# A rank-one matmul for the output bias in place of a GpSimd addition, with the residual loaded into the output tile and the weight loads spread differently (8 cores, one Trainium2 chip)

## The chip, the cores and the metric

The kernel runs on the eight cores of one Trainium2 chip. Each core takes two of the 16 sequences and works alone; nothing is exchanged. The metric is the device time in microseconds (us) of the slowest core. Before the change the median of three runs is 1172.06 us (1171.53 to 1172.96).

TensorE (PE in the profile; PEld is its weight load) multiplies into banks of PSUM, DVE is VectorE, ACT is ScalarE, POOL is GpSimd, and SP is the sync engine that only starts DMAs. Each works through a list of its own in order; semaphores join the lists.

## The reference

One layer over x of shape 16 x 2048 x 1024, float32:

```
xn  = layernorm(x)                                  # no scale, no shift
# branch 1
n   = xn * rsqrt(max(sum(xn*xn), 1e-12))            # rows of length one
sim = n @ n.T                                       # 2048 x 2048 for each sequence
c   = softplus(sum(relu(sim), axis=-1) @ W1 + b1)   # 2048 x 1024
a   = concat([xn, c]) @ W2                          # W2 is 2048 x 1024
# branch 2
P   = xn @ U1                                       # rank 256
H   = gelu(P @ V1 + fb1)                            # 4096 wide
f   = H @ U2 @ V2 + b2
out = x + a + f
```

## The kernel before, in words

A core works on its two sequences ("batches" b = 0 and 1), each in four tiles of 512 tokens (t), each of four blocks of 128 tokens (s_; st = 4t + s_ numbers the 16 blocks). All matmuls are in bfloat16 and mostly 512 columns wide.

An operation is recorded by `A(stream, ...)` with what it reads and writes; `Sched` derives the semaphore waits and appends it to the list of its engine: T is TensorE, V is DVE, S is ACT, G is GpSimd, SY is SP. So the order in which the recording calls are made is the order on every engine. That order comes from `mix`: it takes several lists of (cost, function), and plays next the first unit of the list whose played cost is the smallest share of that list's total. A cost has no other effect.

The stages of a batch in `batch_steps` (sg = 1 to 5) mix these lists:

- `sim_tile_units`: similarity blocks, eight matmuls each (L461), evacuated by DVE with ReLU and row sum (L469), and column sums over a block by a matmul with a 128 x 1 column of ones (L487).
- `cf_unit`: the row of sums is spread to all partitions by a matmul of one row of ones in float32 (L539), and ACT computes softplus from it as Exp (L545) and Ln (L550), eight of each.
- `ffn_units`: P (L570), then 32 steps of H (two matmuls, L587, and a Gelu on ACT, L593) and Q (two matmuls, L599).
- `fin_units`: the output. For each block of 128 tokens: a GpSimd DMA loads x again into `xr` (L626), GpSimd adds b2, which is held spread over all partitions in `b2b`, and writes the sum to `xb` (L631), which is the first weight stage buffer, `wstage[0]`, used again. Then for each half of 512 output columns 18 matmuls into one bank: eight with xn (L640), eight with softplus (L648), two with V2 (L655). DVE adds bank and `xb` into `outsb` (L661), and a GpSimd DMA stores `outsb` (L667). There are 64 such halves, 32 in a batch.
- `prep_units2`: GpSimd DMAs load x into the same two `xr` buffers (L413) for the normed tokens of the next tile (DVE L418, transposed by TensorE L365, copied by DVE L369).
- `wrest` (b = 0, sg = 1 alone): the last 12 of 18 weight chunks. A chunk is an SP DMA of 1 MB into one of two stage buffers (L295), and a cast to bfloat16, on ACT for even chunks (L298, `wstage[0]`) and on DVE for odd ones (L301, `wstage[1]`). Softplus uses `wstage[1]` for its middle result too.

The banks of similarity, column sums and output groups are two (`s0`, `s1`) that take turns. Batch 0's last output tile is mixed with similarity blocks of batch 1; batch 1's last output tile stands alone at the end (the tail).

Of the kernel before, what the change touches and what calls it, by code (L numbers as in the profile page):

```python
# [8 lines left out]
BF16 = mybir.dt.bfloat16  # L9
# [148 lines left out]
def build_program():  # L158
# [13 lines left out]
    b2 = nc.dram_tensor("b2", [1, 1024], F32, kind="ExternalInput")  # L172
# [4 lines left out]
    def sb(name, shape, dt=F32):  # L177
        return es.enter_context(nc.sbuf_tensor(name, shape, dt))
# [13 lines left out]
    b2b = sb("b2b", [128, 1024])  # L192
    onesf = sb("onesf", [1, 128])
    onesb = sb("onesb", [128, 1], BF16)
    identbf = sb("identbf", [128, 128], BF16)
# [5 lines left out]
    xb = [wstage[0][:, 0:1024], wstage[0][:, 1024:2048]]  # L201
# [15 lines left out]
    for n in ["sum", "ssq", "mean", "var", "u", "ru", "sq", "rs", "rs2",  # L217
# [15 lines left out]
                 + [("QXS", i) for i in range(2)]  # L233
                 + [("QTN", i) for i in range(2)]
# [10 lines left out]
    def pool_slot():  # L245
        i = state["pool"] % 2
        state["pool"] += 1
        return pool[i], ("ps", i)

    def vj_slot():  # L250
# [14 lines left out]
    b2bc, _ = bass.broadcast_tensor_aps(b2[0:1, :], b2b[:, :])  # L265
    A("SY", lambda e: e.dma_start(out=b2b[:, :], in_=b2bc),
      writes=[("b2b",)], chan="QC", dma=True)
    A("V", lambda e: e.memset(onesf[:, :], 1.0), writes=[("onesf",)])
    A("V", lambda e: e.memset(onesb[:, :], 1.0), writes=[("onesb",)])

# [350 lines left out]
    def fin_units(b, t):  # L621
        units = []
        for s_ in range(4):
            st = 4 * t + s_
            def gx(st=st):
                A("G", lambda e: e.dma_start(out=xr[st % 2][:, :],  # L626
                                             in_=x[b, st * 128:(st + 1) * 128, :]),
                  writes=[("xr", st % 2)], chan=("QXR", st % 2), dma=True)
            units.append((0, gx))
            def gadd(st=st):  # L630
                A("G", lambda e: e.tensor_tensor(out=xb[st % 2][:, :], in0=xr[st % 2][:, :],  # L631
                                                 in1=b2b[:, :], op=AluOpType.add),
                  reads=[("xr", st % 2), ("b2b",)], writes=[("xb", st % 2), ("wstage", 0)])
            units.append((0, gadd))
            for h in range(2):
                def finh(s_=s_, st=st, h=h):
                    bank, bkey = pool_slot()
                    for dc in range(DC):
# [4 lines left out]
                                   start=(dc == 0), stop=False),  # L643
# [9 lines left out]
                    for rc in range(2):  # L653
# [8 lines left out]
                                      in0=bank[:, :], in1=xb[st % 2][:, h * 512:(h + 1) * 512],  # L662
                                      op=AluOpType.add),
                      reads=[bkey, ("xb", st % 2)], writes=[("outsb", st % 2)])
# [47 lines left out]
    wrest = wunits[6:]  # L712
# [142 lines left out]
```

How the kernel before makes its waits and increments, by code:

```python
    def emit(self, stream, eng, sems):  # L112
        for o in self.streams[stream]:
            if o.drain:
                eng.drain()
            for c, idx in sorted(o.waits.items(), key=lambda kv: str(kv[0])):
                v = self.wait_value(c, idx)
                if v > 0:
                    eng.wait_ge(sems[c], v)
            inst = o.fn(eng)
            if o.marked:
                if inst is None:
                    inst = eng.nop()
                inst.then_inc(sems[o.chan], 16 if o.dma else 1)
# [690 lines left out]
        @block.gpsimd  # L815
        def _(eng):
            sch.emit("G", eng, sems)
            for k in range(3):
                n_store = sch.chan_count.get(("QST", k), 0)
                if n_store:
                    eng.wait_ge(sems[("QST", k)], 16 * n_store)
```

## Time and profile before

| | |
|---|---|
| median of three runs | 1172.06 us |
| the profiled execution | 1172.41 us |
| its span on the slowest core (core 1) | 1170.6 us |
| spans of the eight cores | 1160.8 to 1170.6 us |
| TensorE busy | 803.3 us (69%) |
| weight loads of TensorE | 337.7 us (29%) |
| ACT busy | 360.1 us (31%) |
| DVE busy | 314.2 us (27%) |
| GpSimd busy | 141.1 us (12%) |
| mean granted TensorE clock, core 1 | 0.833 of 2.4 GHz |
| memory traffic | 93.60 MB, mean 80 GB/s |

The stretches, as the windows and the timeline show them for batch 0: until about 165 us the first similarity pass, to 283 us the rest of the weights beside the first FFN tile, to 590 us the mixed stretches with output tiles, to 627 us transposes of batch 1, and until about 700 us the last output tile. Batch 1 repeats the middle part and ends with the tail from 1117 us.

How to read it: times are us, an instruction's mean is ns. "Idle before <- X" is the time for which the engine stood before the instruction and what ended it. A timeline row with xN is a run of N like instructions; its start is the first one's, its duration reaches to the end of the last.

### The profile page before, as it was taken

Reading aid. Unit: us, or ns where it says so; the run is one execution under the profiler, and the core shown is the slowest. Engines: PE = TensorE matmul, PEld = TensorE weight load, DVE = VectorE, ACT = ScalarE, POOL = GpSimd, SP = SyncE. Lnnn points to the kernel's source line nnn. Section 1 sums busy time; section 2 is a strip of 40 time slices with the busy share of each in tenths; the row PEclk is TensorE's granted clock in tenths of the full one; section 3 lists DMA queues with packets and bytes.
Section 4 is the critical chain, followed back from the end, with each engine's and each line's share of the span. In section 5 each row is a group of like instructions: output and inputs, shape, how many; then the busy total and the mean of one; then the engine's idle time right before and its main releaser. Section 6 shows DMA issues by size and latency. Waiting matters only on the chain.

```text
span 1170.6 us, 10338 instructions; the slowest of 8 cores (1160.8 to 1170.6 us)
## 1 busy us (share of the span) xinstructions
PE 803.3 (69%) x3528; PEld 337.7 (29%) x3528; DVE 314.2 (27%) x651; ACT 360.1 (31%) x501; POOL 141.1 (12%) x160
## 2 busy tenths in 40 slices
PE   1454361695699549849948864595789577959983
PEld 0221120232243214323433322132334223423431
DVE  4534421342133212231152343122211211121010
ACT  3233205460633064435300000542332134325300
POOL 0000010001111211111211111000112110211122
PEclk9965675797799779959958976798789898979997
DMA  4123014661233223312261221000112121211131
GB/s 148 54 72 108 13 63 141 220 247 36 73 108 108 72 85 100 122 36 63 100 198 55 90 90 37 18 18 18 55 41 86 36 71 38 72 37 45 64 107 55
DMA packets 30322, 93.60 MB, mean 80 GB/s; under 512 B 4160, under 2 KB 9408, under 8 KB 29760
## 3 DMA queue, kind: packets, MB, share of 16 engines
q1 hardware_dynamic: 16000, 44.69, 12.3%
q0 software_dynamic: 14272, 48.26, 11.9%
q8 instruction: 29, 0.48, 0.2%
q14 instruction: 21, 0.17, 0.0%
HBM read 76.14 MB, written 16.78 MB: 79 GB/s over the span
## 4 chain that ended last, share of the span: by engine, by line
PE 58%; DMA 11%; ACT 11%; DVE 9%; issue 8%; POOL 1%; DVEq 0%; SPq 0%; ACTq 0%; POOLq 0%
PE s L461 13%; PE q L599 11%; PE s L640 8%; PE s L648 8%; PE s L587 5%; PE hx L587 4%; DMA cscr<-crow 4%; ACT wstage L545 4%; PE tb L365 4%; DMA xr<-x 4%; ACT nfm L550 3%; PE s L655 2%; DVE xnfm L369 1%; DVE nfm L369 1%; PE s L487 1%
## 5 line engine op out<-in xcount | busy, mean ns | idle before, releaser
L599 PE MATMUL q<-hbf,u2sb 128*128 128x512 bf16 x512 | 155.3, 385 | 88.6 <-ACT hbf L593 64.6
L461 PE MATMUL s<-nfm 128*128 128x512 bf16 x640 | 183.5, 440 | 9.3 <-DVE outsb L661 4.8
L593 ACT ACTIVATE hbf<-s,fb1c 128x512 bf16<-128x512 f32 x128 | 87.9, 687 | 277.5 <-PE s L587 277.5
L661 DVE TENSOR_TENSOR outsb<-s,wstage 128x512 f32<-128x512 f32 x64 | 44.2, 691 | 368.5 <-PE s L655 242.6
L640 PE MATMUL s<-w2sb,xnfm 128*128 128x512 bf16 x512 | 130.9, 402 | 8.5 <-DVE outsb L661 8.5
L365 PE MATMUL tb<-identbf,xntok 128*128 128x128 bf16 x384 | 44.3, 287 | 121.7 <-DVE xnfm L369 97.9
L593 ACT ACTIVATE hbf<-hx,fb1c 128x512 bf16<-128x512 f32 x128 | 87.9, 686 | 127.2 <-PE hx L587 127.0
L648 PE MATMUL s<-w2sb,nfm 128*128 128x512 bf16 x512 | 123.6, 385 | 0.0
L469 DVE TENSOR_SCALAR_CACHE_REDUCE vjunk<-s 128x512 bf16<-128x512 f32 x80 | 55.3, 691 | 182.5 <-PE s L461 182.5
L461 PEld LDWEIGHTS s<-nfm 128*128 128x128 bf16 x640 | 67.0, 109 | 106.0 <-issue 56.1
L631 POOL TENSOR_TENSOR wstage<-xr,b2b 128x1024 f32<-128x1024 f32 x32 | 74.9, 2341 | 159.3 <-DMA xr<-x 159.3
L587 PE MATMUL s<-pfm,v1sb 128*128 128x512 bf16 x256 | 77.5, 385 | 22.6 <-DVE pfm L576 22.6
L599 PEld LDWEIGHTS q<-hbf,u2sb 128*128 128x128 bf16 x512 | 38.9, 97 | 178.5 <-issue 159.0
L587 PE MATMUL hx<-pfm,v1sb 128*128 128x512 bf16 x256 | 76.6, 381 | 0.0
L640 PEld LDWEIGHTS s<-w2sb,xnfm 128*128 128x128 bf16 x512 | 51.9, 102 | 77.8 <-issue 25.0
L365 PEld LDWEIGHTS tb<-identbf,xntok 128*128 128x128 bf16 x384 | 34.3, 128 | 131.4 <-issue 130.3
L648 PEld LDWEIGHTS s<-w2sb,nfm 128*128 128x128 bf16 x512 | 51.1, 100 | 63.9 <-issue 6.2
L365 PE MATMUL tb<-identbf,ntok 128*128 128x128 bf16 x128 | 16.2, 306 | 72.9 <-ACT ntok L394 61.6
L545 ACT ACT_TABLE_LOAD x8 | 10.3, 1283 | 181.8 <-PE s L539 181.7
L667 POOL DMA_DIRECT2D out<-outsb x32 | 17.8, 557 | 375.7 <-DVE outsb L661 375.7
L526 POOL DMA_DIRECT2D cscr<-crow x32 | 15.8, 495 | 355.7 <-DVE crow L522 315.8
L545 ACT ACTIVATE wstage<-s,b1c,w1c 128x512 f32<-128x512 f32 x64 | 49.8, 778 | 5.6 <-ACT nfm L550 0.4
(86 smaller groups left out, 598.0 us busy)
## 6 DMA issues: line engine op xcount, KB each, us to landing
xr<-x POOLq DMA_DIRECT2D x60, 512.0 KB, 4.9
xa<-x SPq DMA_DIRECT2D x38, 512.0 KB, 4.2
out<-outsb POOLq DMA_DIRECT2D x32, 512.0 KB, 3.0
wstage<-W SPq DMA_DIRECT2D x8, 1024.0 KB, 6.4
wstage<-U SPq DMA_DIRECT2D x5, 1024.0 KB, 6.7
wstage<-V SPq DMA_DIRECT2D x5, 1024.0 KB, 5.9
xr<-x SPq DMA_DIRECT2D x6, 512.0 KB, 5.0
outsb<-x SPq DMA_DIRECT2D x4, 512.0 KB, 8.2
```

The lines of the kernel that those rows point to most:

```text
L365: e.transpose(tb[:, dc * 128:(dc + 1) * 128], src[:, dc * 128:(dc + 1) * 128], identbf[:, :]),
L461: e.matmul(bank[:, :], nfm[:, dc * 2048 + q * 128: dc * 2048 + (q + 1) * 128], nfm[:, dc * 2048 + kc * 512: dc * 2048 + (kc + 1) * 512], s ...
L469: e.tensor_scalar(out=vjunk[:, vs * 512:(vs + 1) * 512], in0=bank[:, :], scalar1=0.0, scalar2=None, op0=AluOpType.max, op1=AluOpType.add, ...
L545: e.activation(out=e512[dc % 2][:, :], in_=s2[:, :], func=AFT.Exp, scale=w1c[:, dc:dc + 1], bias=b1c[:, dc:dc + 1]),
L550: e.activation(out=nfm[:, dc * 2048 + t * 512: dc * 2048 + (t + 1) * 512], in_=e512[dc % 2][:, :], func=AFT.Ln, bias=1.0, scale=1.0),
L587: e.matmul(bank[:, :], v1sb[:, c * 4096 + fc * 128:c * 4096 + (fc + 1) * 128], pfm[t % 2][:, c * 512:(c + 1) * 512], start=(c == 0), stop= ...
L593: e.activation(out=hbf[fc % 2][:, :], in_=bank[:, :], func=AFT.Gelu_apprx_tanh, scale=1.0, bias=fb1c[:, fc:fc + 1]),
L599: e.matmul([q0, q1][rc][:, :], u2sb[:, fc * 256 + rc * 128: fc * 256 + (rc + 1) * 128], hbf[fc % 2][:, :], start=(fc == 0), stop=(fc == 31)),
L631: A("G", lambda e: e.tensor_tensor(out=xb[st % 2][:, :], in0=xr[st % 2][:, :], in1=b2b[:, :], op=AluOpType.add), reads=[("xr", st % 2), (" ...
L640: e.matmul(bank[:, :], xnfm[t % 2][:, dc * 512 + s_ * 128: dc * 512 + (s_ + 1) * 128], w2sb[:, dc * 1024 + h * 512: dc * 1024 + h * 512 + ...
L648: e.matmul(bank[:, :], nfm[:, dc * 2048 + t * 512 + s_ * 128: dc * 2048 + t * 512 + (s_ + 1) * 128], w2sb[:, (8 + dc) * 1024 + h * 512: (8 ...
L661: e.tensor_tensor(out=outsb[st % 2][:, h * 512:(h + 1) * 512], in0=bank[:, :], in1=xb[st % 2][:, h * 512:(h + 1) * 512], op=AluOpType.add),
```

## The change

Three edits. The matmul: b2 is loaded as one row, cast to bfloat16, and added inside the output group by a 19th matmul, a row of ones (1 x 128) against a row of b2 (1 x 512), which opens the group. The residual: x is loaded into the output tile `outsb` itself, and DVE adds the bank to it in place; the GpSimd addition and the buffer `xb` are gone, and the load unit has a cost of 600 instead of 0. The weights: to `wrest` is added a unit that does nothing and costs as much as all others together.

```diff
@@ -189,16 +189,16 @@
     w1c = sb("w1c", [128, 8])
     b1c = sb("b1c", [128, 8])
     fb1c = sb("fb1c", [128, 32])
-    b2b = sb("b2b", [128, 1024])
+    b2bf = sb("b2bf", [1, 1024], BF16)
     onesf = sb("onesf", [1, 128])
     onesb = sb("onesb", [128, 1], BF16)
+    onesbr = sb("onesbr", [1, 128], BF16)
     identbf = sb("identbf", [128, 128], BF16)
     identf = sb("identf", [128, 128])
 
     nfm = sb("nfm", [128, 8 * 2048], BF16)
     xa = [sb(f"xa{i}", [128, 1024]) for i in range(2)]
     xr = [sb(f"xr{i}", [128, 1024]) for i in range(2)]
-    xb = [wstage[0][:, 0:1024], wstage[0][:, 1024:2048]]
     outsb = [sb(f"outsb{i}", [128, 1024]) for i in range(2)]
     xnfm = [sb(f"xnfm{i}", [128, 8 * 512], BF16) for i in range(2)]
     ntok = [sb(f"ntok{i}", [128, 1024], BF16) for i in range(2)]
@@ -231,6 +231,7 @@
     dma_chans = (["QC"] + [("QW", i) for i in range(2)] + [("QXA", i) for i in range(2)]
                  + [("QXR", i) for i in range(2)] + [("QXO", i) for i in range(2)]
                  + [("QXS", i) for i in range(2)]
+                 + [("QXF", i) for i in range(2)]
                  + [("QTN", i) for i in range(2)]
                  + [("QST", i) for i in range(3)])
     sch = Sched(streams, total_chans=["QC"])
@@ -262,11 +263,13 @@
       writes=[("b1c",)], chan="QC", dma=True)
     A("SY", lambda e: e.dma_start(out=fb1c[:, :], in_=fb1[:, :]),
       writes=[("fb1c",)], chan="QC", dma=True)
-    b2bc, _ = bass.broadcast_tensor_aps(b2[0:1, :], b2b[:, :])
-    A("SY", lambda e: e.dma_start(out=b2b[:, :], in_=b2bc),
-      writes=[("b2b",)], chan="QC", dma=True)
+    A("SY", lambda e: e.dma_start(out=crow1[0:1, 0:1024], in_=b2[0:1, :]),
+      writes=[("crow1", 0), ("crow1", 1)], chan="QC", dma=True)
+    A("V", lambda e: e.tensor_copy(b2bf[0:1, :], crow1[0:1, 0:1024]),
+      reads=[("crow1", 0), ("crow1", 1)], writes=[("b2bf",)])
     A("V", lambda e: e.memset(onesf[:, :], 1.0), writes=[("onesf",)])
     A("V", lambda e: e.memset(onesb[:, :], 1.0), writes=[("onesb",)])
+    A("V", lambda e: e.memset(onesbr[:, :], 1.0), writes=[("onesbr",)])
 
     def weight_units():
         chunks = []
@@ -623,24 +626,23 @@
         for s_ in range(4):
             st = 4 * t + s_
             def gx(st=st):
-                A("G", lambda e: e.dma_start(out=xr[st % 2][:, :],
+                A("G", lambda e: e.dma_start(out=outsb[st % 2][:, :],
                                              in_=x[b, st * 128:(st + 1) * 128, :]),
-                  writes=[("xr", st % 2)], chan=("QXR", st % 2), dma=True)
-            units.append((0, gx))
-            def gadd(st=st):
-                A("G", lambda e: e.tensor_tensor(out=xb[st % 2][:, :], in0=xr[st % 2][:, :],
-                                                 in1=b2b[:, :], op=AluOpType.add),
-                  reads=[("xr", st % 2), ("b2b",)], writes=[("xb", st % 2), ("wstage", 0)])
-            units.append((0, gadd))
+                  writes=[("outsb", st % 2)], chan=("QXF", st % 2), dma=True)
+            units.append((600, gx))
             for h in range(2):
                 def finh(s_=s_, st=st, h=h):
                     bank, bkey = pool_slot()
+                    A("T", lambda e:
+                      e.matmul(bank[:, :], onesbr[:, :],
+                               b2bf[0:1, h * 512:(h + 1) * 512], start=True, stop=False),
+                      reads=[("onesbr",), ("b2bf",)], writes=[bkey], tag=f"Fb2_{b}_{t}_{s_}")
                     for dc in range(DC):
                         A("T", lambda e, dc=dc:
                           e.matmul(bank[:, :],
                                    xnfm[t % 2][:, dc * 512 + s_ * 128: dc * 512 + (s_ + 1) * 128],
                                    w2sb[:, dc * 1024 + h * 512: dc * 1024 + h * 512 + 512],
-                                   start=(dc == 0), stop=False),
+                                   start=False, stop=False),
                           reads=[("xnfm", t % 2), ("w", "w2")],
                           writes=[bkey], tag=f"F{b}_{t}_{s_}")
                     for dc in range(DC):
@@ -659,9 +661,10 @@
                           reads=[("qfm", t % 2), ("w", "v2")], writes=[bkey])
                     A("V", lambda e:
                       e.tensor_tensor(out=outsb[st % 2][:, h * 512:(h + 1) * 512],
-                                      in0=bank[:, :], in1=xb[st % 2][:, h * 512:(h + 1) * 512],
+                                      in0=bank[:, :],
+                                      in1=outsb[st % 2][:, h * 512:(h + 1) * 512],
                                       op=AluOpType.add),
-                      reads=[bkey, ("xb", st % 2)], writes=[("outsb", st % 2)])
+                      reads=[bkey, ("outsb", st % 2)], writes=[("outsb", st % 2)])
                 units.append((9600, finh))
             def store(st=st):
                 A("G", lambda e: e.dma_start(out=out[b, st * 128:(st + 1) * 128, :],
@@ -709,7 +712,7 @@
 
     play(startup)
     play(wunits[:6])
-    wrest = wunits[6:]
+    wrest = wunits[6:] + [(sum(c for c, _ in wunits[6:]), lambda: None)]
 
     def batch_steps(b):
         nxt = b + 1
```

Where it moves instructions. First, ACT in the first FFN tile of batch 0, from the last Ln of softplus. `hbf` is the Gelu's output from the banks `s3` and `hx`, `w2sb` and `u2sb` are bfloat16 weights. Before:

```order
L550 ACTIVATE nfm<-wstage1 128x512
L593 ACTIVATE hbf0<-s3,fb1c 128x512
L593 ACTIVATE hbf1<-hx,fb1c 128x512
L593 ACTIVATE hbf0<-s3,fb1c 128x512
L298 CAST u2sb<-wstage0 128x2048
L593 ACTIVATE hbf1<-hx,fb1c 128x512
L593 ACTIVATE hbf0<-s3,fb1c 128x512
L593 ACTIVATE hbf1<-hx,fb1c 128x512
L593 ACTIVATE hbf0<-s3,fb1c 128x512
L593 ACTIVATE hbf1<-hx,fb1c 128x512
L593 ACTIVATE hbf0<-s3,fb1c 128x512
L298 CAST w2sb<-wstage0 128x2048
```

And now:

```order
L553 ACTIVATE nfm<-wstage1 128x512
L301 CAST u2sb<-wstage0 128x2048
L596 ACTIVATE hbf0<-s3,fb1c 128x512
L596 ACTIVATE hbf1<-hx,fb1c 128x512
L596 ACTIVATE hbf0<-s3,fb1c 128x512
L301 CAST w2sb<-wstage0 128x2048
L596 ACTIVATE hbf1<-hx,fb1c 128x512
L596 ACTIVATE hbf0<-s3,fb1c 128x512
L596 ACTIVATE hbf1<-hx,fb1c 128x512
L301 CAST w2sb<-wstage0 128x2048
```

The first cast has moved ahead of the first Gelu, and three Gelus instead of six stand between two casts. Five ACT casts follow softplus in both; the last now has 12 Gelus ahead of it and 20 behind, where it had 27 and 5.

Second, GpSimd in the first mixed stretch with an output tile. `xr<-x` at L413 (now L416) is the load for the next tile's normed tokens. Before:

```order
L626 DMA xr<-x 128x1024
L631 TENSOR_TENSOR wstage<-xr,b2b 128x1024
L413 DMA xr<-x 128x1024
L667 DMA out<-outsb 128x1024
L626 DMA xr<-x 128x1024
L631 TENSOR_TENSOR wstage<-xr,b2b 128x1024
L413 DMA xr<-x 128x1024
```

And now:

```order
L629 DMA outsb<-x 128x1024
L416 DMA xr<-x 128x1024
L670 DMA out<-outsb 128x1024
L629 DMA outsb<-x 128x1024
L416 DMA xr<-x 128x1024
```

The addition is gone; the order of loads and stores is the same, and the load of a block goes into the buffer whose store is two stores back.

Third, TensorE in the tail, two groups on the banks `s0` and `s1`. Before:

```order
L640 MATMUL s0<-w2sb,xnfm1 128x512 x8
L648 MATMUL s0<-w2sb,nfm 128x512 x8
L655 MATMUL s0<-v2sb,qfm1 128x512 x2
L640 MATMUL s1<-w2sb,xnfm1 128x512 x8
L648 MATMUL s1<-w2sb,nfm 128x512 x8
L655 MATMUL s1<-v2sb,qfm1 128x512 x2
```

And now:

```order
L637 MATMUL s0<-b2bf,onesbr 128x512
L642 MATMUL s0<-w2sb,xnfm1 128x512 x8
L650 MATMUL s0<-w2sb,nfm 128x512 x8
L657 MATMUL s0<-v2sb,qfm1 128x512 x2
L637 MATMUL s1<-b2bf,onesbr 128x512
L642 MATMUL s1<-w2sb,xnfm1 128x512 x8
L650 MATMUL s1<-w2sb,nfm 128x512 x8
L657 MATMUL s1<-v2sb,qfm1 128x512 x2
```

Each group has one matmul more in front.

## Rows read from the trace of the kernel before

**Rows 1.** The page: the span and the engines' busy time with shares.

```profile
span 1170.6 us, 10338 instructions; the slowest of 8 cores (1160.8 to 1170.6 us)
...
PE 803.3 (69%) x3528; PEld 337.7 (29%) x3528; DVE 314.2 (27%) x651; ACT 360.1 (31%) x501; POOL 141.1 (12%) x160
```

**Rows 2.** Windows: length, busy us of five engines, clock, DMA share, GB/s.

```profile
215.00:265.00 50.00, 49.05 (x207) 18.68 (x205) 19.61 (x38) 29.26 (x35) 1.23 (x2) 0.96 0.66 230
540.00:590.00 50.00, 47.92 (x219) 19.39 (x216) 7.79 (x12) 17.87 (x26) 10.33 (x9) 1.00 0.30 93
```

**Rows 3.** Waits, whole span: who waited for whom, us in total, times, longest.

```profile
DVE outsb L661 <- POOL wstage L631: 122.3, 15, 11.6
...
PE s L640 <- DVE outsb L661: 8.5, 3, 3.5
...
PE s L461 <- DVE outsb L661: 4.8, 5, 2.2
```

**Rows 4.** Timeline of ACT in the weight stretch: start, us, line, operation, [idle before].

```profile
206.53 1.28 ACT L593 ACT_TABLE_LOAD   x1
...
216.38 1.90 ACT L298 CAST u2sb<-wstage 128x2048 bf16<-128x2048 f32 x1 [0.16 <-PE q L599]
...
247.06 1.89 ACT L298 CAST w2sb<-wstage 128x2048 bf16<-128x2048 f32 x1
...
256.97 1.89 ACT L298 CAST w2sb<-wstage 128x2048 bf16<-128x2048 f32 x1
...
264.61 0.69 ACT L593 ACTIVATE hbf<-hx,fb1c 128x512 bf16<-128x512 f32 x1 [0.40 <-PE hx L587]
```

**Rows 5.** The weight loads' line (L295), its eight W2 loads, 218 to 256 us.

```profile
DMA to landing us min/median/max: 4.8/6.4/8.5
```

**Rows 6.** The same line, the two U2 loads issued at 206.59 and 207.00 us.

```profile
DMA to landing us min/median/max: 5.5/6.9/8.2
```

**Rows 7.** Timeline of TensorE: its restart in the weight stretch.

```profile
213.56 1.01 PE L599 MATMUL q<-hbf,u2sb 128*128 128x512 bf16 x2 [17.91 <-DVE u2sb L301]
```

**Rows 8.** Timeline of TensorE around a column sum (L487) and around L539.

```profile
226.80 0.59 PE L599 MATMUL q<-hbf,u2sb 128*128 128x512 bf16 x2
227.32 0.38 PE L487 MATMUL s<-vjunk,onesb 128*1 128x512 bf16 x1
227.63 0.39 PE L461 MATMUL s<-nfm 128*128 128x512 bf16 x1
...
295.15 0.59 PE L587 MATMUL s<-pfm,v1sb 128*128 128x512 bf16 x2 [1.01 <-DVE pfm L576]
295.67 1.12 PE L539 MATMUL s<-crow,onesf 1*128 1x512 f32 x2
296.73 0.61 PE L640 MATMUL s<-w2sb,xnfm 128*128 128x512 bf16 x2
```

**Rows 9.** Timeline of TensorE: the wait behind softplus, batch 1, second tile.

```profile
852.60 1.01 PE L599 MATMUL q<-hbf,u2sb 128*128 128x512 bf16 x2 [9.19 <-ACT hbf L593]
```

**Rows 10.** Timeline, batch 0's last output tile: GpSimd's addition and two waits of TensorE.

```profile
636.71 2.33 POOL L631 TENSOR_TENSOR wstage<-xr,b2b 128x1024 f32<-128x1024 f32 x1 [6.75 <-DMA xr<-x]
...
640.06 3.57 PE L640 MATMUL s<-w2sb,xnfm 128*128 128x512 bf16 x8 [3.49 <-DVE outsb L661]
...
659.19 3.54 PE L461 MATMUL s<-nfm 128*128 128x512 bf16 x8 [2.21 <-DVE outsb L661]
```

**Rows 11.** Timeline of the tail: first group, a wait, last addition, last store.

```profile
1117.16 1.89 PE L640 MATMUL s<-w2sb,xnfm 128*128 128x512 bf16 x8
...
1145.82 1.89 PE L640 MATMUL s<-w2sb,xnfm 128*128 128x512 bf16 x8 [2.44 <-DVE outsb L661]
...
1155.12 1.49 DVE L661 TENSOR_TENSOR outsb<-s,wstage 128x512 f32<-128x512 f32 x2 [8.66 <-POOL wstage L631]
...
1157.18 0.57 POOL L667 DMA_DIRECT2D out<-outsb  x1 [2.23 <-DVE outsb L661]
```

**Rows 12.** Timeline of DVE at the start: statistics of two blocks of x.

```profile
11.95 1.22 DVE L439 TENSOR_SCALAR_CACHE_REDUCE ntok<-xa 128x1024 bf16<-128x1024 f32 x1 [0.58 <-DMA xa<-x]
...
13.74 1.22 DVE L439 TENSOR_SCALAR_CACHE_REDUCE ntok<-xr 128x1024 bf16<-128x1024 f32 x1 [0.56 <-DMA xr<-x]
```

## The prediction, as put on record before the result

> **What bounds the kernel now.** I read the page first. TensorE is busy 69% of the span and every other engine under a third [rows 1], so I asked the windows where TensorE is full. In the stretch where batch 0 runs its first FFN tile while the last weights load, it is busy 49.05 of 50 us; in the last mixed stretch of batch 0, 47.92 of 50 us [rows 2]. There an added matmul shows in full. The windows also say what the weight stretch does to memory: 230 GB/s, the DMA engines busy 0.66. It is full on TensorE and close to full on DMA.
>
> Then the waits. DVE stood 122.3 us in front of its output addition (L661) because GpSimd's x+b2 (L631) was late, but TensorE waited for that addition only 8.5 + 4.8 us [rows 3]. Most of the 122.3 us is idle time of an engine that nobody needs. The places where TensorE does wait are at two stretches of four token tiles: the last output tile of batch 0 (x from 627 us) and the tail (from 1117 us). So the removed addition has a small price to give back, and I look for the cost in the two other edits: the matmul for b2 and the doubled pace of the weight loads.
>
> **Part A: the weights come at double pace.** The empty unit appended to `wrest` doubles that list's total, so `mix` has spent all 12 weight units when the other lists stand at half. On ACT a weight cast now follows every three Gelus instead of every six, and the first one stands ahead of the first Gelu. Before, two casts were 256.97 − 247.06 = 9.9 us apart with six Gelus between them, 1.65 us for each Gelu of the stage, TensorE full [rows 4]. Each ACT cast frees stage buffer 0, whose next load then takes 6.4 us to land (median of the eight W2 loads; 4.8 at best, 8.5 at worst) [rows 5], and the cast itself 1.9 us. With 0.2 us for the issue one turn of the buffer is 8.5 us. That fits into 9.9 us; it does not fit into the 3 × 1.65 = 4.95 us that three Gelus give.
>
> The sum: the first such load is issued at 207.00 and lands after 8.2 us [rows 6], at 215.2; its cast ends at 217.1. Four more turns of 8.5 us: the last ACT cast ends at 251.1. Twelve Gelus are then done, 20 are left. Two start at once (0.9 us for the first), the other 18 follow at 1.65: the last one starts at 251.1 + 0.9 + 29.7 = 281.7. It started at 264.61 [rows 4], so +17.1 us. TensorE restarts each turn after some 4 us of idleness; where it did so before, eight matmuls took 3.54 us for the usual 1.9 [rows 10]. During the turns that lies in the wait; after the last it adds 1.7. I take +19.
>
> Bounds: if no turn is bound by its load, only the late start is left: Gelu 1 starts after 217.1 and a table load of 1.28 [rows 4], and TensorE, which resumed at 213.56 [rows 7], resumes at 219.1: +5.5. If each turn costs 10.4 us (8.5 landing, 1.9 cast), it is 7.6 more: +27. A load in this stretch also shares the engines with two x loads, which is why I don't go lower than the median.
>
> The skill speaks for a cheaper turn. The Trainium skill, "DMA: Bandwidth & Descriptors", section Specifications, gives a limit of about 358 GB/s per core from HBM. By it the two loads of a turn would need only 5.9 us, 2.6 less than my turn, and this part would come out at 19 − 4 × 2.6 = +8.6, an estimate; this trace doesn't show it: its fullest stretch moved 230 GB/s [rows 2], and the sum goes by the landing times.
>
> **Part B: 64 matmuls for b2.** One row by 128 columns of ones against a row of b2, 512 columns, before each of the 64 output groups. Its cost is the time between starts. Ordinary matmuls of 512 columns start 0.216 us apart: eight take 1.89 us [rows 11], of which the last one's own 0.38 is to be taken off, over seven starts. The trace has two kinds that use less than the full array. The column-sum (L487, one output column): the pair before it starts at 226.80, it starts at 227.32, the next at 227.63; so 0.52 − 0.216 = 0.31 on the way in and 0.31 on the way out. The nearest in shape is L539, one row of ones too: 295.15 to 295.67 is again 0.52, 0.31 on the way in; out of it 295.67 to 296.73, 1.06 for its two f32 halves, which I read as twice 0.43 (each two passes of 0.216) and about 0.1 behind each half [rows 8]. So a b2 matmul adds 0.31 + 0.31 − 0.216 = 0.40 us, at 2.4 GHz. Lower end 0.216 (nothing at the borders); upper end 0.62 (the array at 1.2 GHz for all of it, twice 0.31). I take 0.40 since both rows agree on the way in.
>
> The Trainium skill, "TensorEngine Tiling (Array Packing)", section Key Properties, says that a change of the tiling mode drains TensorE. By this rule a one-row matmul between full ones costs a drain twice, which is the extra 0.09 at each side in rows 8; without it the part would be the 0.216 end.
>
> Of 64, 48 stand in the six mixed stretches (two of them behind L539, while TensorE is about to wait 9.19 us for ACT anyway [rows 9], and cost nothing): 46 × 0.40 = +18.4. Eight stand in batch 0's last output tile, eight in the tail; they are in part C.
>
> **Part C: the GpSimd addition goes.** x is loaded straight into the output tile, and DVE adds the bank to it in place: same shape, same time. GpSimd's 2.34 us leaves the path from the load's landing to DVE's addition. The load must now wait until the last store of that output buffer, two tiles earlier, has landed; it stands behind the next tile's store in the same queue anyway, a whole tile later, so this costs nothing. The queue order of stores and loads stays.
> Batch 0's last output tile: TensorE waited 3.49 us and 2.21 us for the addition, and after each eight matmuls ran at half clock (3.57 and 3.54 us for 1.9) [rows 10]. The load landed at 636.7, so the first wait shrinks to 1.1 and the second goes: −4.6. The slow matmuls I count at half of 3.3: −1.7. The eight b2 matmuls cost +3.2. Together −3.1.
> Tail: before, from the first group at 1117.16 to the last store at 1157.18 it is 40.0 us, with two waits of about 2.5 us and the last double addition, held by GpSimd, at 1155.12 [rows 11]. Now a group takes 18 × 0.216 + 0.40 = 4.29, eight take 34.3; then 0.3 to DVE, 0.69 for one addition (the other half is done by then), 0.57 to the store: 35.9. The load is no longer late: DVE was idle for 8.66 us before 1155.12; without GpSimd's 2.34 and 0.2 between, x is there 6.1 us behind the last addition of the tile before, and the bank that waits for it is wanted 8.6 us behind it. So −4.1.
>
> **Part D: the start.** The b2 broadcast of 512 KB leaves the queue ahead of x; loads of that size land 1.8 us apart (11.95 to 13.74) [rows 12]. DVE now has to wait for the small constants and convert b2, about 1 us, which ends before the first x lands. −1.5 (0 to −1.8).
>
> **Sum.** +19 + 18.4 − 3.1 − 4.1 − 1.5 = +28.7 us. The profiled execution took 1172.4 (1.8 around its span), 0.35 above the median of the three, which is nothing at this size: 1172.4 + 28.7 = 1201, of which I shave one for b2 matmuls that fall into small waits (0.6 to 1 us each where TensorE waits for a Gelu): 1200.
>
> **Rivals.**
> 1. The weights keep up (part A at its lower end): the loads' landing times include queueing that goes away when both buffers turn evenly. For it: 4.8 us at best, DMA engines only 0.66 busy. Against: the turn is a chain of load, cast and issue, and even 4.8 + 1.9 is over 4.95. 1200 − 12 = 1188.
> 2. The b2 matmul costs its 0.216 only, since bf16 with 128 columns loads its weights as its neighbours do: 62 × 0.19 less: 1200 − 12 = 1188. Against: the way into L539.
> 3. Faster. DVE's 122.3 us of head-of-line waits hold work behind them (evacuations of similarity blocks, FFN casts), and with them gone TensorE stays at full clock in the last tiles. Its place is the mixed and last output stretches, its price at most all 13.3 us of waits, 5 of half clock, and 4.5 at the end of the tail; with D −24. It decides only if A costs under 6 and B under 14 (0.216 each); then 1172.4 − 24 + 5.5 + 13.4 = 1167. Against: TensorE is full where most of those waits lie.
> 4. The pace does not change the load order as read (a unit with nothing in it is played and ignored): the rows on ACT exclude it.
>
> **Chances.** Forecast as told (1194 to 1208) 0.52; rival 1 or 2 alone (1184 to 1194) 0.28; dearer than told, with turns of 10 us or b2 matmuls at half clock (1208 to 1220), 0.10; both rivals together or better, 1174 to 1184, 0.04; rival 3 0.05, no change 0.01. Range 1185 to 1212. Faster than by 0.2% (2.3 us, about what a measurement here can tell) 0.05, within it 0.02, slower 0.93.
>
> **What would show it.** Weight casts on ACT about 8.5 us apart between 215 and 252 with three Gelus between them, ACT idle until "DMA wstage" before them; TensorE at about 60% in that stretch; the stage's last Gelu near 282. Starts of b2 matmul and neighbours 0.31 apart on both sides. Tail from its first group to the last store near 36 us with no TensorE wait for DVE. Wrong would be: ACT casts 5 us apart, TensorE above 90% there, or b2 matmuls 0.22 apart.

## The result, and the profile after

The changed kernel takes 1192.79 us (median of eight runs, 1191.41 to 1194.46); the kernel before took 1171.94 beside it. The ratio is 1.0176, 95% interval 1.0165 to 1.0187: slower by 20.9 us. The forecast was 1200 within 1185 to 1212. In some executions of each kernel the cores of one die or of both show a lower granted clock and the time is longer (one of the changed kernel: 1271.47 us); times and ratios here are of the others.

The page of the slowest core, core 3, answers to [rows 1]:

```profile
span 1191.9 us, 10392 instructions; the slowest of 8 cores (1184.6 to 1191.9 us)
...
PE 823.1 (69%) x3592; PEld 336.2 (28%) x3592; DVE 313.6 (26%) x653; ACT 359.7 (30%) x501; POOL 64.5 (5%) x128
```

TensorE has 64 matmuls and 20 us of busy time more, GpSimd 77 us less (12% to 5%), and the other shares are nearly as before. A page can't say where 21 us went. So I cut each core's time at landmarks that both kernels have: the first of the four transfers of each row-sum (L526, now L529), the casts of Q (L616) that end the fourth FFN tile, and the last store. The table gives the time between landmarks in us, the median of the eight cores of the profiled run. "Mixed" is the sum of the six mixed stretches, 48 output groups; "last tile, batch 0" has in it also the transposes and first similarity blocks of batch 1.

| | to first row-sum | first FFN tile (weights) | mixed | last tile, batch 0 | batch 1, first tile | tail |
|---|---|---|---|---|---|---|
| before | 161.2 | 106.0 | 628.6 | 125.8 | 92.4 | 39.8 |
| changed | 159.1 | 122.0 | 644.0 | 122.5 | 92.2 | 36.0 |
| difference | −2.1 | +16.0 | +15.4 | −3.3 | −0.2 | −3.8 |
| forecast | −1.5 | +19 | +18.4 | −3.1 | 0 | −4.1 |

The differences add to +22.0. Sign and place of all four parts are as forecast; the size of the one in batch 0's last tile needs a second look, which it gets under e5 and e9.

**The weight stretch.** Windows of the changed kernel; the first answers to the first of [rows 2], where TensorE was busy 49.05 of 50 us:

```profile
215.00:265.00 50.00, 39.91 (x146) 14.26 (x145) 16.14 (x30) 21.21 (x25) 1.05 (x2) 0.83 0.63 207
213.00:249.00 36.00, 25.91 (x88) 9.23 (x88) 10.54 (x18) 16.18 (x19) 1.05 (x2) 0.78 0.84 270
```

While the loads run, TensorE is busy 72% (some 60% was forecast) and the DMA engines move 270 GB/s. The timeline of ACT there, its five weight casts, the first Gelu and the stretch's last, answers to [rows 4]:

```profile
209.17 1.88 ACT L301 CAST u2sb<-wstage 128x2048 bf16<-128x2048 f32 x1
211.07 1.28 ACT L596 ACT_TABLE_LOAD   x1
212.37 0.69 ACT L596 ACTIVATE hbf<-s,fb1c 128x512 bf16<-128x512 f32 x1
...
218.48 1.90 ACT L301 CAST w2sb<-wstage 128x2048 bf16<-128x2048 f32 x1 [2.64 <-DMA wstage<-W]
...
227.97 1.90 ACT L301 CAST w2sb<-wstage 128x2048 bf16<-128x2048 f32 x1 [5.05 <-DMA wstage<-W]
...
235.41 1.90 ACT L301 CAST w2sb<-wstage 128x2048 bf16<-128x2048 f32 x1 [2.16 <-DMA wstage<-W]
...
243.89 1.90 ACT L301 CAST w2sb<-wstage 128x2048 bf16<-128x2048 f32 x1 [4.04 <-DMA wstage<-W]
...
278.47 0.69 ACT L596 ACTIVATE hbf<-hx,fb1c 128x512 bf16<-128x512 f32 x1 [0.40 <-PE hx L590]
```

Each of the last four casts stood waiting for its load, and they are 9.3, 9.5, 7.4 and 8.5 us apart, with three Gelus between: 34.7 us for four turns, where 34.0 was forecast (34.6 to 37.0 over the eight cores). The line of the weight loads gives, for its eight W2 loads, against [rows 5]:

```profile
DMA to landing us min/median/max: 5.3/7.0/8.2
```

**The b2 matmul.** TensorE's timeline near the end of the last mixed stretch:

```profile
1133.82 0.59 PE L602 MATMUL q<-hbf,u2sb 128*128 128x512 bf16 x2
1134.34 0.39 PE L637 MATMUL s<-b2bf,onesbr 1*128 1x512 bf16 x1
1134.66 0.82 PE L642 MATMUL s<-w2sb,xnfm 128*128 128x512 bf16 x3
```

It starts 0.52 after a pair and the next one 0.32 after it, as in [rows 8]. Over 128 of them (two cores) the median is 0.310 in and 0.317 out; so it adds 0.41 us where 0.40 was forecast.

**The tail.** Two halves of one block and the last store, to set beside [rows 11]:

```profile
1158.27 0.69 DVE L663 TENSOR_TENSOR outsb<-s,outsb 128x512 f32<-128x512 f32 x1 [6.16 <-DMA outsb<-x]
...
1160.03 0.69 DVE L663 TENSOR_TENSOR outsb<-s,outsb 128x512 f32<-128x512 f32 x1 [1.08 <-PE s L657]
...
1178.53 0.54 POOL L670 DMA_DIRECT2D out<-outsb  x1 [7.56 <-DVE outsb L663]
```

The load still lands after the first half's matmuls are done, but before its bank is wanted, so TensorE no longer stops: from the first group at 1142.56 to the last store 36.0 us, forecast 35.9. In the list of waits the 122.3 us and the two TensorE rows of [rows 3] have become the second and third of these:

```profile
DVE outsb L663 <- PE s L657: 350.5, 61, 26.3
DVE outsb L663 <- DMA outsb<-x: 18.5, 3, 6.3
PE s L464 <- DVE outsb L663: 2.6, 4, 0.6
```

The first of these rows was, before:

```profile
DVE outsb L661 <- PE s L655: 242.6, 45, 25.1
```

So DVE waits 104 us less for x, and 108 us more for TensorE: it stands as long as before, for something else. The two stretches where TensorE had waited are 7 us shorter.

### The profile page after: what moved, and what is told of

The parts are those of the page before. It is cut to its first block, busy times and chain, and to the rows that moved or that the text cites. A ratio compares the mean times of both kernels' runs of the same rounds, so it can differ in the third digit from the quotient of the medians.

```text
span 1191.9 us, 10392 instructions; the slowest of 8 cores (1184.6 to 1191.9 us)
## 1 busy us (share of the span) xinstructions
PE 823.1 (69%) x3592; PEld 336.2 (28%) x3592; DVE 313.6 (26%) x653; ACT 359.7 (30%) x501; POOL 64.5 (5%) x128
## 4 chain that ended last, share of the span: by engine, by line
PE 63%; DMA 10%; DVE 9%; ACT 9%; issue 8%; DVEq 0%; SPq 0%; ACTq 0%; POOL 0%; POOLq 0%
PE s L464 13%; PE s L642 10%; PE q L602 10%; PE s L650 9%; PE s L590 4%; DMA cscr<-crow 4%; PE hx L590 4%; PE tb L368 4%; ACT wstage L548 3%; ACT nfm L553 2%; PE s L657 2%; DMA wstage<-W 2%; PE s L637 2%; DVE xnfm L372 1%; PE s L573 1%
## 5 line engine op out<-in xcount | busy, mean ns | idle before, releaser
L663 DVE TENSOR_TENSOR outsb<-s,outsb 128x512 f32<-128x512 f32 x64 | 44.3, 692 | 368.9 <-PE s L657 350.5
L642 PE MATMUL s<-w2sb,xnfm 128*128 128x512 bf16 x512 | 125.6, 389 | 0.0
L650 PE MATMUL s<-w2sb,nfm 128*128 128x512 bf16 x512 | 121.8, 381 | 0.0
L642 PEld LDWEIGHTS s<-w2sb,xnfm 128*128 128x128 bf16 x512 | 45.7, 99 | 64.1 <-issue 20.9
L494 DVE TENSOR_TENSOR crow<-crow,s 1x512 f32<-1x512 f32 x48 | 32.2, 674 | 49.8 <-PE s L490 49.8
L590 PEld LDWEIGHTS s<-pfm,v1sb 128*128 128x128 bf16 x256 | 24.5, 99 | 67.6 <-issue 41.0
```

The source lines that it names most:

```text
L494: e.tensor_tensor(out=crow1[0:1, kc * 512:(kc + 1) * 512], in0=crow1[0:1, kc * 512:(kc + 1) * 512], in1=bank[0:1, 0:512], op=AluOpType.add),
L590: e.matmul(bank[:, :], v1sb[:, c * 4096 + fc * 128:c * 4096 + (fc + 1) * 128], pfm[t % 2][:, c * 512:(c + 1) * 512], start=(c == 0), stop= ...
L642: e.matmul(bank[:, :], xnfm[t % 2][:, dc * 512 + s_ * 128: dc * 512 + (s_ + 1) * 128], w2sb[:, dc * 1024 + h * 512: dc * 1024 + h * 512 + ...
L650: e.matmul(bank[:, :], nfm[:, dc * 2048 + t * 512 + s_ * 128: dc * 2048 + t * 512 + (s_ + 1) * 128], w2sb[:, (8 + dc) * 1024 + h * 512: (8 ...
L663: e.tensor_tensor(out=outsb[st % 2][:, h * 512:(h + 1) * 512], in0=bank[:, :], in1=outsb[st % 2][:, h * 512:(h + 1) * 512], op=AluOpType.add),
```

## The experiments

Ratios are to the kernel before on the same chip. "As e1" and so on refer to the labels. The theory has three parts: A, the stage buffer's turn (load, cast, issue) is longer than three Gelus; B, a one-row matmul costs its 0.216 us and 0.1 at each change between full rows and one row; C, what the late load and addition cost is seen only where TensorE waits for them. e2, e3 and e4 are set beside e1, which came 7 us over its own forecast; so their times are read as differences from it.

**e1: the pace undone.**

```diff
-    wrest = wunits[6:] + [(sum(c for c, _ in wunits[6:]), lambda: None)]
+    wrest = wunits[6:]
```

> The changed kernel with the weight loads at their old pace (the empty unit left off). Theory A (the doubled pace makes the first FFN tile wait for its weight loads): the stretch from the first row-sum transfer to the second is 17 us shorter, as before the change, and the kernel takes 1192.8 - 16.8 = 1176 us, about 4 us over the kernel before. Rival (the pace is hidden and the whole loss is the b2 matmuls, 64 of them with cold starts at 0.4 us or more): no change, above 1188 us.

Measured: 1182.85 us, ratio 1.0083 (1.0052 to 1.0113). The first FFN tile fell from 122.0 to 107.7 us, 14.3 us; the kernel by 10 us against a run on another chip. The rival is out; the forecast was 7 us too low. The four runs of e1 scatter more (1180.0 to 1185.6; nine of e2 on the same chip 1171.0 to 1173.2). In the profiled one the slowest core was 4 us behind the next, and the second mixed stretch of batch 1 took 111.8 us for the 109.9 of the changed kernel with the same code in it. The windows of core 1 show that stretch in both; the last three columns are clock, DMA share and GB/s. Changed kernel:

```profile
939.20:1049.00 109.80, 81.78 (x358) 33.23 (x359) 16.98 (x32) 35.71 (x50) 8.23 (x17) 0.88 0.17 58
```

And e1:

```profile
926.00:1037.80 111.80, 83.51 (x359) 33.56 (x360) 16.99 (x32) 35.71 (x50) 8.31 (x17) 0.86 0.17 57
```

The same matmuls, but the granted clock is 0.86 for 0.88: more of them fell into stretches at the lower clock. It is no scatter of single cores: the stretch took 109.8 to 109.9 us on all eight cores of the changed kernel, in both of its profiled executions, and 111.8 on all eight of e1. Such differences of 2 us come and go between kernels with the same order there, and no part of the forecast could have them.

**e5 and the changed kernel again: the pace alone, on one chip.** e5 has the reverse edit of e1 in the kernel before, and nothing else.

> The kernel before with nothing changed but the pace of the weight loads (the empty unit added). Theory A: the stretch between the first and the second row-sum transfer is 17 us longer and so is the kernel, 1172 + 17 = 1189 us; with the loads at hand nothing later gains from it. Rival (undoing the pace gave only 10 us on another chip, so 10 is its worth, and the rest comes back in later stretches): 1182 us.

> The changed kernel as it is, on the chip of the next runs, since undoing the pace gave 10 us less time and not 17, measured on another chip than this kernel's 1192.8. If the chips differ: about 3 to 6 us more here against the same kernel before (ratio 1.020 to 1.023). If not: ratio 1.0176 again, and the missing 6 us have another cause.

Measured: e5 1186.82 us, ratio 1.011 (1.0068 to 1.0152); the changed kernel again 1197.38 us, ratio 1.0188 (1.0149 to 1.0226), the same as at first within its interval, so one change of chip left its ratio as it was. The changed kernel was not run on e1's own chip, so what part of e1's 7 us is the chip isn't shown. In e5 the first FFN tile grew from 106.0 to 122.4 us, +16.4, beside +16.0 in the changed kernel. Its ACT casts (core 6) have the changed kernel's waits:

```profile
209.84 1.88 ACT L298 CAST u2sb<-wstage 128x2048 bf16<-128x2048 f32 x1
220.17 1.90 ACT L298 CAST w2sb<-wstage 128x2048 bf16<-128x2048 f32 x1 [3.65 <-DMA wstage<-W]
229.81 1.90 ACT L298 CAST w2sb<-wstage 128x2048 bf16<-128x2048 f32 x1 [5.20 <-DMA wstage<-W]
236.87 1.90 ACT L298 CAST w2sb<-wstage 128x2048 bf16<-128x2048 f32 x1 [1.78 <-DMA wstage<-W]
247.19 1.90 ACT L298 CAST w2sb<-wstage 128x2048 bf16<-128x2048 f32 x1 [5.88 <-DMA wstage<-W]
```

The kernel's +13 (8 to 18 by the interval) holds both the 17 and the rival's 10. By stretches A is there in full; its last output tile of batch 0 was 3.4 us shorter (122.4 for 125.8), which the theory has no reason for. TensorE's waits for the output addition are 6.6 us there in both (median core); the granted clock is 0.81 in the kernel before and 0.83 in e5. So the 3.4 us is not in those waits; that it is chance of the clock is likely, not shown: before, the eight cores range from 121.2 to 127.8 us there, in e5 from 119.5 to 128.0.

**e6: a pace between.** On e2, an empty unit of a quarter.

```diff
-    wrest = wunits[6:]
+    wrest = wunits[6:] + [(sum(c for c, _ in wunits[6:]) // 4, lambda: None)]
```

> As e2 (full-array b2 matmul), with an empty unit of a quarter of the list's cost, so the loads come 1.25 times as fast: four or five Gelus between two ACT casts instead of six (old pace) or three (changed kernel). Theory A (a turn of the stage buffer, load 6.4 us + cast 1.9 us + issue = 8.5 us, is the bound; five Gelus of 1.65 us give 8.25 us): four turns short by 0.25 us, the first stretch at most 2 us longer than in e2 (108.0 us), 1173 us. Rival (loss in proportion to how far the loads are moved ahead; they are moved 40% as far as in the changed kernel, which cost 16 us): +6 us.

Measured: 1174.23 us, ratio 1.0004 (0.9992 to 1.0017), 2.6 us over e2 (0.9991), on another chip. The first FFN tile took 111.7 us, +3.7 on e2's 108.0: between the two expectations. In the slowest core only one of the five casts waits for its load, for 0.90 us, so most of the 3.7 is not the turn as I described it. The cores range from 106.8 to 114.4 us, and they go in the main with the granted clock of the stretch: two at 0.79 took 106.9 and 107.6 us (e2's four at 0.79: 106.4 to 106.8), one at 0.78 109.5 (e2's four at 0.78: 109.3 to 109.9), and four at 0.76 to 0.77, which no core of e2 has, 111.2 to 114.3; but one at 0.79 took 112.1. So much of the 3.7 is time at the lower clock; why there was more of it stays open.

**e2 and e3: what makes a b2 matmul dear.** e2, on e1, fills the rows:

```diff
-    b2bf = sb("b2bf", [1, 1024], BF16)
+    b2bf = sb("b2bf", [128, 1024], BF16)
-    onesbr = sb("onesbr", [1, 128], BF16)
+    onesbr = sb("onesbr", [128, 128], BF16)
+    A("V", lambda e: e.memset(b2bf[:, :], 0.0), writes=[("b2bf",)])
...
-                               b2bf[0:1, h * 512:(h + 1) * 512], start=True, stop=False)
+                               b2bf[:, h * 512:(h + 1) * 512], start=True, stop=False)
```

> As e1, but the b2 matmul uses all 128 rows: 128 x 128 ones against a tile whose row 0 is b2 and whose other rows are zero. Theory B (what makes a b2 matmul dear is going from full rows to one row and back): it starts 0.216 us from its neighbours on both sides instead of 0.31 each, 62 exposed ones give 62 x 0.2 = 12.6 us back, 1163.5 us. Rival (an added matmul costs what it costs, whatever its rows): as e1, 1176 us.

e3, on e1, issues the one-row matmul twice:

```diff
-    A("V", lambda e: e.memset(onesbr[:, :], 1.0), writes=[("onesbr",)])
+    A("V", lambda e: e.memset(onesbr[:, :], 0.5), writes=[("onesbr",)])
...
+                    A("T", lambda e:
+                      e.matmul(bank[:, :], onesbr[:, :],
+                               b2bf[0:1, h * 512:(h + 1) * 512], start=False, stop=False),
```

> As e1, but two one-row matmuls in each group, each with ones of 0.5, so the sum is the same. Theory B (the cost is at the borders between one row and full rows): the second costs only 0.216 us, 62 x 0.216 = +13.4 over e1, 1189.5 us. Rival (every one-row matmul costs 0.42 by itself): +26 us over e1, 1202 us.

Measured: e2 1171.62 us, ratio 0.9991 (0.9978 to 1.0004), 11 us under e1 (forecast 12.6). e3 1204.29 us, ratio 1.0262 (1.0225 to 1.0299), 21 us over e1, between the two and nearer the rival's 26. The starts decide. e2's b2 matmul in the tail:

```profile
1142.34 0.59 PE L658 MATMUL s<-v2sb,qfm 128*128 128x512 bf16 x2
1142.77 0.38 PE L638 MATMUL s<-b2bf,onesbr 128*128 128x512 bf16 x1
1142.98 1.89 PE L643 MATMUL s<-w2sb,xnfm 128*128 128x512 bf16 x8
```

And e3's two:

```profile
1168.87 0.59 PE L661 MATMUL s<-v2sb,qfm 128*128 128x512 bf16 x2
1169.40 0.38 PE L637 MATMUL s<-b2bf,onesbr 1*128 1x512 bf16 x1
1169.62 0.37 PE L641 MATMUL s<-b2bf,onesbr 1*128 1x512 bf16 x1
1169.93 1.90 PE L646 MATMUL s<-w2sb,xnfm 128*128 128x512 bf16 x8
```

With 128 rows, 0.215 on either side. With one row, 0.31 in, 0.226 between the two, 0.307 out (medians of 128): the second costs 0.226, the borders the rest. The Trainium skill's rule ("TensorEngine Tiling (Array Packing)", Key Properties: a change of the tiling mode drains TensorE) agrees with these starts in all three kernels, if a one-row matmul is taken for a change of mode, which the section doesn't say. That the borders are what costs is shown by e2 and e3; what happens at a border no trace shows. But 64 × 0.226 is 14.5 us, and e3's stretches grew by 20.2 in all. Of the 5.7 us more, 2.7 are in batch 0's last tile, which grew by 4.5 us for eight such matmuls, with the granted clock at 0.81 where e1 has 0.84; the rest is in the mixed stretches (14.6 for 10.8), and I can't place it.

**e4: no b2 matmul.** On e1, the matmul's lines deleted and `start=(dc == 0)` back in the first group.

> As e1, without the b2 matmul and with nothing in its place; this leaves b2 out of the result. It shows what the direct load of x and the missing GpSimd addition give alone. Theory: 62 x 0.42 = 26 us under e1, 1150 us, 22 us under the kernel before (start 2.6, batch 0's last output tile 8.4, tail 7.5, and about 3 unaccounted). Rival (the b2 matmuls lie largely beside other waits, under 0.25 us each): above 1160 us.

Measured: 1160.61 us, ratio 0.9888 (0.986 to 0.9917), 22 us under e1 (forecast 26). By its time alone this is at the rival's border, above 1160; the stretches decide. The mixed stretches took 628.1 us, as before the change (628.6) and 18.0 less than e1's 646.1: for 46 exposed matmuls, 0.39 us each, 18.4 had been forecast. That is not the rival's 0.25. The last tile of batch 0 took 117.9 (before 125.8) and the tail 33.0 (before 39.8). So without b2 the direct load, the missing addition and the shorter start are together worth 13 to 14 us.

**e9 and e10: GpSimd's addition, late or ahead.** e9 puts it back on e4, in place:

```diff
+            def gadd(st=st):
+                A("G", lambda e: e.tensor_tensor(out=outsb[st % 2][:, :], in0=outsb[st % 2][:, :],
+                                                 in1=b2b[:, :], op=AluOpType.add),
+                  reads=[("outsb", st % 2), ("b2b",)], writes=[("outsb", st % 2)])
+            units.append((0, gadd))
```

> As e4 (x loaded into the output tile, no b2 matmul, old pace), with GpSimd's addition of b2 back, in place in the output tile, behind the load in the same queue. Theory C (what the removed addition gives is its 2.34 us between the landing and the bank's release, which TensorE sees in batch 0's last output tile and in the tail): the mixed stretches as in e4, the tail back from 33.0 to 39.8 us, the last output tile of batch 0 back by 5 us or more, 1160.6 + 12 = 1172 us, and e10's gain is the lead of a block. Rival (the shared x buffers were the cause): as e4, 1161 us.

e10 is the kernel before with the load and the addition of block st + 2 recorded right after the store of block st, in two buffers of their own use, the halves of the first weight stage buffer:

```diff
+        def resid(st):
+            def gx():
+                A("G", lambda e: e.dma_start(out=xb[st % 2][:, :],
+                                             in_=x[b, st * 128:(st + 1) * 128, :]),
...
+            def gadd():
+                A("G", lambda e: e.tensor_tensor(out=xb[st % 2][:, :], in0=xb[st % 2][:, :],
+                                                 in1=b2b[:, :], op=AluOpType.add),
...
+            return [(0, gx), (0, gadd)]
+        units.extend(resid(4 * t) + resid(4 * t + 1))
...
+            if s_ < 2:
+                units.extend(resid(st + 2))
```

> The kernel before, with GpSimd's x + b2 kept but loaded and added one block ahead, straight into the two halves of the first weight stage buffer (in place), and the b2 broadcast moved behind the first six loads of x. No b2 matmul, old pace. Theory C (what the old form lost was the lateness of the load and of the addition, behind the store in one queue; the addition itself is free): no wait of TensorE for the output addition, the last output tiles and the start as in e4, so e4's time or a little less: 1160 us. Rival (GpSimd's addition also costs by itself, through shared access to memory): 1165 us or more.

Measured: e9 1172.08 us, ratio 0.9993 (0.9979 to 1.0006), as the kernel before and as forecast; its tail is back at 39.8 us and its last tile of batch 0 at 121.8, 3.9 us over e4 where 5 or more had been forecast. In the tail TensorE waited 4.6 us for the output addition before, 4.4 in e9 and 0.1 in e4 (median core): there the shared x buffers were not the cause. In batch 0's last tile these waits are 6.6 us before, but 3.2 in e9 and 2.6 in e4. So there only 0.6 of the 4.1 us came back with the addition. The loads of x land there 4.8 us after their issue in e9 and in e4, 6.0 before (medians); whether the buffer or the moment of the load does that, no run separates. e10 1162.47 us, ratio 0.9905 (0.9868 to 0.9942), with a tail of 32.6 us. In its tail GpSimd adds while DVE and TensorE work, and after its first output addition DVE waits for TensorE alone:

```profile
1122.03 0.69 DVE L661 TENSOR_TENSOR outsb<-s,wstage 128x512 f32<-128x512 f32 x1 [2.50 <-PE s L655]
1122.45 2.35 POOL L628 TENSOR_TENSOR wstage<-wstage,b2b 128x1024 f32<-128x1024 f32 x1 [3.26 <-DMA wstage<-x]
1124.74 0.57 POOL L667 DMA_DIRECT2D out<-outsb  x1
1125.85 0.69 DVE L661 TENSOR_TENSOR outsb<-s,wstage 128x512 f32<-128x512 f32 x1 [3.13 <-PE s L655]
```

DVE's addition takes 0.69 us beside it as elsewhere; over the eight cores 28 of them lie wholly beside one of GpSimd's. Part C is shown for the tail: 2.34 us of work was free and its place in the queue was not. The mixed stretches (628.0) and the tail are as in e4. Batch 0's last tile is not: 121.5 us for e4's 117.9, with waits of 3.2 us and a granted clock of 0.80 (e4: 2.6 and 0.83), and the forecast had them equal. So b2 added ahead costs at most the 2 us by which e10 is over e4, which their intervals cover, while the cheapest b2 matmul (e2) costs 11 us over e4.

**e8: softplus with a buffer of its own.** On e2:

```diff
-    e512 = [wstage[1][:, 0:512], wstage[1][:, 512:1024]]
+    e512 = [sb(f"e512_{i}", [128, 512]) for i in range(2)]
...
-                  writes=[("e512", dc % 2), ("wstage", 1)])
+                  writes=[("e512", dc % 2)])
...
-                  reads=[("e512", dc % 2), ("wstage", 1)], writes=[("nfm", t)],
+                  reads=[("e512", dc % 2)], writes=[("nfm", t)],
```

> As e2 (old pace, full-array b2 matmul), and softplus keeps its middle result in a buffer of its own instead of the second weight stage buffer, so that the next U2 chunk is loaded and cast while softplus runs. Theory (in the kernel before TensorE stood 17.9 us until that chunk's cast at 213.6; what is left to wait for is the first Gelu behind softplus, 5 us earlier): the first stretch 5 us shorter, 1167 us where e2 has 1171.7. Rival (that wait is softplus alone): as e2.

Measured: 1158.82 us, ratio 0.9863 (0.9818 to 0.9907), 13 us under e2 by the times, on two chips, and 15 by the ratios and by the stretches; the first FFN tile 100.5 us for 108.0, 7.5 less where 5 were forecast. TensorE's restart, after [rows 7]:

```profile
207.97 1.01 PE L603 MATMUL q<-hbf,u2sb 128*128 128x512 bf16 x2 [12.37 <-ACT hbf L597]
```

It now waits for the first Gelu behind softplus instead of for a weight cast. The edit does a second thing, which the forecast did not have: each Exp had written, and each Ln read, the one entry `("wstage", 1)`, so an Exp could not start until the Ln before it was done. ACT in softplus, e2 and then e8:

```profile
195.04 0.63 ACT L554 ACTIVATE nfm<-wstage 128x512 bf16<-128x512 f32 x1
195.76 0.78 ACT L549 ACTIVATE wstage<-s,b1c,w1c 128x512 f32<-128x512 f32 x1
```

```profile
195.35 0.63 ACT L554 ACTIVATE nfm<-e 128x512 bf16<-128x512 f32 x1
195.89 0.76 ACT L549 ACTIVATE e<-s,b1c,w1c 128x512 f32<-128x512 f32 x1
```

The next Exp starts 0.54 us after the Ln instead of 0.72, and from the first Exp to the eighth a softplus takes 9.74 us for 11.15. There are eight of them, and TensorE's wait behind one falls by the same 1.4 us (8.97 to 7.56 in batch 0's second tile). So 1.4 of the 7.5 us in the first tile are this; the mixed stretches are 6.7 us shorter in all, and batch 1's first tile 1.1.

**e11: both.**

> e10 and e8 together: no b2 matmul, GpSimd's addition a block ahead, softplus with a buffer of its own (a small row buffer moved to unused partitions of another to make room). The two gains lie in different stretches: e8's first stretch was 7.5 us shorter than e2's, so e10's 1162.5 - 7.5 = 1155 us, 1.6% under the kernel before. Rival (both shorten the same wait): 1160 us.

Measured: 1145.14 us, ratio 0.9771 (0.9731 to 0.9811); first FFN tile 101.7 us, tail 32.6. The gains add and more (1155 was forecast): the mixed stretches are 5.9 us shorter than e10's, the shorter softplus of e8, which the forecast had left out. It beats the kernel before by 2.3% (1.9 to 2.7) and the changed one by 4%.

## Why the prediction was right

The time is inside the range, and the four parts are where they were forecast. It is not in the band called "as told" (1194 to 1208) but in the one given to rival 1 or 2 alone (1184 to 1194), and neither of them held: A and B were both there, each 3 us smaller than forecast.

- **What bounds the kernel.** TensorE, at these places. e4's mixed stretches equal those before although GpSimd's addition, for which DVE had waited 122.3 us, is gone: right, for the mixed stretches.
- **Part A, the weights.** Forecast +19, measured +16.0 in the median of the cores, +16.4 alone in e5. The turn was right: 34.7 us for four (34.0) on the slowest core, at most 37.0 on the others. The first term was not: I let the first load start at 207.00 as before, since softplus used the stage buffer ahead of it. But two chunks are now recorded before softplus, their loads start at 186.9 and 192.3 and land in 6.9 us, and the first ACT cast ends at 211.1, not 217.1. In exchange DVE casts them ahead of P's evacuation, and TensorE and softplus start later. TensorE's restart at H:

```profile
195.99 1.01 PE L590 MATMUL s<-pfm,v1sb 128*128 128x512 bf16 x2 [25.69 <-DVE pfm L579]
```

It waited 25.69 us there, 16.54 before. Counted from each core's own first row-sum transfer (159.4 here, 163.5 in the profile before) the first cast ended 2.0 us sooner than forecast, and the last Gelu came 17.9 us later than before. The part was worked out on a core whose stretch was among the shortest, 105.3 us (the eight range to 109.2), so 19 meant 124.3; the slowest core after has 123.2 and the median core 122.0. So 1 us was in my steps and 2 in the spread between cores.
- **The Trainium skill's limit of 358 GB/s from HBM** ("DMA: Bandwidth & Descriptors", Specifications) would have made this part +8.6, an estimate. The stretch moved 270 GB/s with the DMA engines busy 0.84, and part A cost 16: here the trace goes against using that limit as the rate of a two-buffer turn.
- **Part B.** 0.41 us each (0.40), +15.4 in the mixed stretches (18.4) by before and after; e4 against e1 gives 18.0. Of the 2.6 us between the two, 2.0 is e1's own length over the changed kernel's, nearly all of it in the stretch of e1's windows, where the granted clock differs. The first mixed stretch shows the same: +1.5 in the changed kernel with the granted clock at 0.90 (before 0.87), +2.6 in e1 at 0.87. The term is right for one matmul; the sum had no term for the clock. Rival 2 (0.216 us) fell with the starts in the trace and with e2.
- **Part C.** The tail, −3.8 (−4.1): right, and e9 shows that it is the lateness of the addition. Batch 0's last output tile, −3.3 (−3.1): the number fits partly by luck. TensorE's waits for the addition fell about as forecast, by 4.1 us (4.6), but e5, which leaves the output path alone, is 3.4 us shorter there too, and in e9, where the addition is back, only 0.6 us of the waits came back with it.
- **Part D.** −2.1 (−1.5), past its own bound of −1.8. The kernels with the same start (e2, e6 and e8 have one small memset more) range from 159.1 to 161.1 us there, so the gain is somewhere from nothing to 2.1.
- **Rival 1** (the weights keep up) is out: all four casts waited. Its own price was a little off: part A at its lower end is 13.5 us less, not 12. **Rival 3** (faster) was priced at 24 us with the start, and e4 gave 13 to 14; its conditions did not hold either.
- **The sum** was 28.7, the stretches give 22.0, the medians 20.9. Of the 7 us, 3 are in A and 3 in B.

## What to carry to other kernels

Before pulling loads forward in a mixed order, compare the turn of the stage buffer (load + cast + issue) with the work that stands between two casts: a cast in an engine's list that waits for its load stops everything behind it. A small addition on an idle engine is free, or nearly (2 us at most here), if it is recorded one block ahead of its user; moving it to the engine that bounds the kernel is not, even as one matmul in nineteen. If a bias must go through TensorE, give it all 128 rows. When a buffer is shared to save room, look at what else its entry in the dependence list orders: here it held back every Exp of softplus.

## What the runs showed of the hardware that was not expected

- A matmul of one row and 128 columns between full ones starts 0.310 us after its predecessor and the next 0.317 after it, against 0.215 with 128 rows (zeros in 127), in 128 instances each. Two one-row matmuls in a row are 0.226 apart.
- The first FFN tile, alone with the doubled pace, moved 270 GB/s over 36 us per core with all eight cores at it, and a 1 MB load still took 7.0 us in the median (5.3 to 8.2), 6.4 before at 230 GB/s.
- The same stretch with the same instructions took 109.8 or 111.8 us with the granted clock at 0.88 or 0.86, in each of the two kernels alike on all eight cores. In e5, which has no b2 matmuls, this stretch took 106.7 us on four cores with the granted clock at 0.87 and 109.2 on the other four at 0.84, in one execution.
